# The second experts in two parts of two sequences

## The chip, the cores and the metric

One core of a Trainium2 chip. The metric is the device time of one execution in microseconds (us). PE is the matrix engine (TensorE), DVE VectorE, ACT ScalarE, POOL GpSimd and SP SyncE, which here only issues DMAs. Each engine works through its own queue in order and waits on counting semaphores.

## The reference

Four sequences of 512 tokens with 128 channels pass two layers. Both layers modulate with values from a conditioning vector (scale, shift and gate per sequence). Layer 0 is a state-space mixer and eight experts with two of eight chosen. Layer 1 is causal attention with 16 heads and a second set of eight experts, which the change is about:

```python
logits = flat @ Wr                                            # 2048 tokens, 8 experts
top_vals, top_idx = jax.lax.top_k(logits, TOP_K)              # TOP_K = 2
weights = jax.nn.softmax(top_vals, axis=-1)
top1 = top_idx[:, 0]
h = jax.nn.gelu(jnp.einsum('td,edh->teh', flat, W1), approximate=False)   # 128 -> 512
y = jnp.einsum('teh,ehd->ted', h, W2)                         # 512 -> 128
out = weights[:, 0] * y[top1]                                 # in short: the best expert's row alone
```

The kernel computes for each token the one best expert e with the weight w = 1 / (1 + exp(second - best)). So each token belongs to one expert, and which one is known only at run time.

## The kernel before, in words

All work of layer 1 follows orders written out by hand, one for each engine.

**The attention** goes in 16 groups of four heads, four per sequence, in a loop over `it` (-2 to 16) with eight slots `i` each. In iteration `it` PE computes the scores of group `it + 2` (`scores`, L1641) for the row maxima, which DVE takes (`maximum`, L1221); POOL splits the maxima of group `it + 1` in three bf16 parts in four small operations (`max_parts`, L522 to L528); PE transposes them in slot 2 (`maxima_T`, L1651), ACT copies them (L817) and SP stores them as extra rows of the queries (L364); and PE computes the transposed scores of group `it` with them subtracted (`scores_T`, L1667, L1672), ACT exponentiates (`probs`, L778), and PE weights the values (`weighted_values`, L1686). A group's output goes through ACT (L811), a transpose (`o_T`, L1695) and a division (`o_norm`, L1233, L1237); after a sequence's four groups come a transpose (`a_T`, L1702), the output projection (`attn_out`, L1710) and the sum into x (L1243). Scores, projections and transposes share three PSUM banks in turn, the ring: a bank is taken again when its reader is done. In iterations 4, 5, 8 and 9 POOL issues the copies of the next sequences' queries and keys (`late_relayout`, L317), two groups of four DMAs per iteration, each after the landing of the one before.

**The router's input** of a sequence is x normalized (`ln_stats`, `ln_moments`, `ln_rstd` L399 and L401, `ln_apply` L406), scaled and shifted (`router_input`). For sequences 0 to 2 POOL does this in iterations 10 to 15, for the last one DVE after the attention.

**The second experts** begin when the attention has ended. PE transposes the input of all four sequences (L1367) and forms the logits (L1509), DVE chooses the largest (L1088 to L1092), and PE counts with two products (L1750, L1751) the rank of each token in its expert. From these DVE works out blocks of 128 rows, each of one expert (at most 16 + 8 - 1 = 23), the place of each token (`posu`) and the expert of each block (L1275 to L1292). POOL stores the 16 tiles of tokens at their places in HBM (L586), SP loads the blocks (L370), and then come 23 blocks:

```python
pool.indirect_dma_start(out=slots_x[:, :], out_offset=bass.IndirectOffsetOnAxis(
    ap=posu[:, t:t + 1], axis=0), in_=rows[:, t, :], in_offset=None).then_inc(sem("scattered"), 16)
...
v.tensor_copy(w1[:, j % 2, :], w["W1"][:, bass.ds(at_w, HID)]).then_inc(sem("w1"), 1)
v.tensor_copy(xT[:, j % 2, :], ps[:, 2 + j % 2, 0:P]).then_inc(sem("xT"), 1)
...
mm = pe.matmul(ps[:, 6 + j % 2, 0:D], gs[:, j % 2, q * P:(q + 1) * P],
               w["W2"][:, bass.ds(at_w[j] + q * D, D)], start=(q == 0), stop=(q == 3))
```

In a block step PE transposes the next block (L1762), computes this one's hidden layer (L1771) and the previous one's output (L1782); ACT applies gelu (L838); DVE copies the next block's weights and input (L1319, L1321) and the previous output (L1325), and a gate row of the first 16 steps (L1329). POOL stores each block's 128 results back by token (L592, the return stores). When all are back, SP loads them (L373), each sequence is multiplied and added (`combine`, L413, L415), and SP stores the output (L381).

## Time and profile before

| | us |
|---|---|
| median of 3 runs (579.58 to 580.09) | 580.0 |
| profiled execution | 577.07 |
| its span, first to last instruction | 575.2 |
| PE busy | 452.4 (79%) |
| DVE busy | 392.0 (68%) |
| ACT busy | 278.1 (48%) |
| POOL busy | 271.6 (47%) |
| mean granted clock of PE, full is 1 | 0.889 |

The span is 1.87 us shorter than the profiled execution's own time, and that execution is 2.9 us below the median of the runs. Busy shares are averages over stages of different kinds; the attention's loop lies roughly between 300 and 463 us, the blocks of the second experts between 510 and 558.

### The profile page before, as it was taken

How to read it: one execution, taken by the hardware profiler on the slowest of the kernel's cores; microseconds unless marked ns; L12 is line 12 of the kernel's file. 1: busy time of each engine (PE TensorE's matmuls, PEld its weight loads, DVE VectorE, ACT ScalarE, POOL GpSimd, SP SyncE). 2: the span in 40 equal slices, each digit the busy share in tenths (PEclk: the TensorE clock that was granted, in tenths of full speed). 3: DMA queues.
4: the chain of work that ended last, by engine and by line, in shares of the span. 5: the costliest groups of instructions: out<-in, count | busy, mean ns of one | idle time of the engine just before them, and what ended most of it. 6: DMA issues, size and time to landing. Idle time of an engine off the chain costs nothing.

```text
span 575.2 us, 10088 instructions
## 1 busy us (share of the span) xinstructions
PE 452.4 (79%) x3120; PEld 274.4 (48%) x3120; DVE 392.0 (68%) x1264; ACT 278.1 (48%) x518; POOL 271.6 (47%) x392
## 2 busy tenths in 40 slices
PE   3688778987998999994558998999999863059970
PEld 3545456766653444442323434435445343049970
DVE  5789738988655888886679687888898235025533
ACT  1568796653453544441223577678777831013220
POOL 4210038998301786664641047476655502714541
PEclk9988889999799999997775799999999985559995
DMA  8600000000335333310386012222300000141114
GB/s 354 169 1 1 0 2 2 1 2 1 144 148 125 99 106 99 107 62 2 108 208 124 4 31 88 82 86 85 84 5 4 3 0 10 52 123 36 36 38 146
DMA packets 25739, 39.94 MB, mean 69 GB/s; under 512 B 3228, under 2 KB 17756, under 8 KB 25164
## 3 DMA queue, kind: packets, MB, share of 16 engines
q1 hardware_dynamic: 21752, 30.42, 17.8%
q0 software_dynamic: 3936, 8.89, 5.2%
q8 instruction: 26, 0.43, 0.3%
q14 instruction: 25, 0.20, 0.1%
HBM read 27.55 MB, written 11.55 MB: 68 GB/s over the span
## 4 chain that ended last, share of the span: by engine, by line
PE 49%; DVE 18%; POOL 11%; issue 8%; ACT 6%; DMA 6%; SPq 0%; DVEq 0%; POOLq 0%; ACTq 0%
PE ps L1579 5%; PE ps L1581 5%; PE ps L1568 5%; PE ps L1686 4%; PE ps L1599 3%; PE ps L1771 3%; PE ps L1782 3%; POOL slots_x L586 3%; DVE rows L406 3%; PE ps L1391 2%; DVE moe L1221 2%; PE ps L1641 2%; POOL qk_parts L305 2%; DVE st L387 2%; PE ps L1672 2%
## 5 line engine op out<-in xcount | busy, mean ns | idle before, releaser
L1221 DVE CUSTOM_DVE_ANT_0 moe<-ps,const 128x512 bf16<-128x512 f32 (+3 forms) x256 | 110.5, 486 | 9.7 <-PE ps L1641 9.4
L778 ACT ACTIVATE arena<-ps 128x256 f32<-128x256 f32 (+3 forms) x128 | 85.8, 701 | 33.6 <-PE ps L1672 32.9
L476 POOL TENSOR_TENSOR arena<-arena 128x512 f32<-128x512 f32 x32 | 51.7, 1616 | 51.9 <-DVE arena L1139 51.7
L1641 PE MATMUL ps<-arena 48*128 48x128 bf16 (+3 forms) x256 | 56.1, 329 | 10.7 <-DVE arena L1221 4.7
L1672 PE MATMUL ps<-arena 51*128 51x128 bf16 (+3 forms) x256 | 52.2, 307 | 0.0
L1686 PE MATMUL ps<-arena 128*32 128x512 f32 (+3 forms) x512 | 48.4, 450 | 0.9 <-ACT arena L778 0.6
L1667 PE MATMUL ps<-bconst 64*128 64x64 bf16 x512 | 45.6, 195 | 1.2 <-ACT arena L778 0.5
L1641 PEld LDWEIGHTS ps<-arena 48*128 48x128 bf16 x256 | 16.7, 97 | 55.7 <-DVE arena L1221 31.7
L751 ACT ACTIVATE arena<-arena 128x512 f32<-128x512 f32 x32 | 20.2, 630 | 41.9 <-DVE arena L1139 41.6
L838 ACT ACTIVATE arena<-ps 128x512 f32<-128x512 f32 x23 | 13.7, 597 | 55.0 <-PE ps L1771 55.0
L592 POOL DMA_INDIRECT tokens_y<-arena,token_at x23 | 22.1, 960 | 32.5 <-DVE arena L1325 31.3
L950 DVE SCALAR_TENSOR_TENSOR arena<-ps,mixw,arena 128x511 f32<-128x511 f32 (+2 forms) x48 | 33.1, 737 | 5.2 <-ACT arena L643 5.2
L1667 PEld LDWEIGHTS ps<-bconst 64*128 64x128 bf16 x512 | 29.5, 97 | 12.0 <-ACT arena L778 4.5
L1579 PE MATMUL ps<-arena,moe 128*128 128x512 f32 x64 | 32.8, 593 | 1.8 <-DVE arena L1122 1.8
L441 POOL TENSOR_TENSOR arena<-arena 128x256 f32<-128x256 f32 x16 | 12.4, 776 | 44.4 <-DVE arena L933 40.5
L1581 PE MATMUL ps<-arena,moe 128*128 128x512 f32 x64 | 32.7, 592 | 0.0
L1568 PE MATMUL ps<-arena,moe 128*128 128x512 f32 x64 | 32.5, 592 | 0.0
L1130 DVE SCALAR_TENSOR_TENSOR arena<-ps,moe,arena 128x512 f32<-128x512 f32 x32 | 24.0, 751 | 12.3 <-PE ps L1581 12.2
L1762 PE MATMUL ps<-const,arena 128*128 128x128 f32 x23 | 6.5, 293 | 29.1 <-DMA arena<-slots_x 29.1
L1367 PE MATMUL ps<-const,rows 128*128 128x128 f32 x64 | 13.8, 367 | 17.6 <-DVE rows L406 14.9
L1771 PE MATMUL ps<-arena 128*128 128x128 f32 x184 | 26.5, 290 | 0.6 <-DVE arena L1321 0.5
L1139 DVE SCALAR_TENSOR_TENSOR arena<-ps,moe,arena 128x512 f32<-128x512 f32 x32 | 24.0, 751 | 3.5
(239 smaller groups left out, 1113.2 us busy)
## 6 DMA issues: line engine op xcount, KB each, us to landing
arena<-expert_weights SPq DMA_DIRECT2D x32, 256.0 KB, 3.2
arena<-moe_in SPq DMA_DIRECT2D x1, 4100.0 KB, 12.8
qk_parts<-arena SPq DMA_DIRECT2D x24, 128.0 KB, 2.3
qk_parts<-arena POOLq DMA_DIRECT2D x24, 128.0 KB, 2.3
arena<-qk_parts POOLq DMA_DIRECT2D x32, 96.0 KB, 2.5
arena<-qk_parts SPq DMA_DIRECT2D x8, 288.0 KB, 5.6
moe<-moe_in SPq DMA_DIRECT2D x1, 1936.0 KB, 13.8
slots_x<-zeros SPq DMA_DIRECT2D x1, 1518.0 KB, 19.6
```

What stands on the lines that cost most here:

```text
L476: pool.tensor_tensor(yacc[:, ts], yacc[:, ts], pr[:, i % 2, :], ALU.add).then_inc(sem("yacc"), 1)
L778: act.activation(pt[:, u % 4, :, 0:n], ps[:, 4 + 2 * k:6 + 2 * k, 0:n], ACT.Exp, scale=ATT_SCALE).then_inc(sem("probs"), 1)
L950: v.scalar_tensor_tensor(out=acc[b % 2][:, c, s:S], in0=ps[:, c, 0:S - s], scalar=w["conv_w"][:, 4 * c + 3 - s:4 * c + 4 - s], in1=acc[b % ...
L1221: v.tensor_tensor_reduce(out=junk[:, done % 2, 0:n], in0=ps[:, k, col:col + n], in1=w["mask"][:, (3 - qt) * P:4 * P], scale=1.0, scalar=3 ...
L1568: pe.matmul(ps[:, 6 + i % 2, :], w["w2"][:, e * D:(e + 1) * D], gT[:, i % 2, :], start=True, stop=True).then_inc(sem("p2_ps"), 1)
L1579: pe.matmul(ps[:, 2 + i % 2, :], w["w1"][:, e * D:(e + 1) * D], xm[:, i % 2, :], start=True, stop=True).then_inc(sem("p1_ps"), 1)
L1581: pe.matmul(ps[:, 4 + i % 2, :], w["w3"][:, e * D:(e + 1) * D], xm[:, i % 2, :], start=True, stop=True).then_inc(sem("p3_ps"), 1)
L1641: mm = pe.matmul(ps[:, k, col:col + n], qaug[lo:lo + KR, b % 2, 2 * g + j // 2, qt * P:(qt + 1) * P], kaug[lo:lo + KR, b % 2, 2 * g + j // ...
L1667: pe.matmul(ps[:, bank, HALF * qh:HALF * (qh + 1)], w["causal"][lo:lo + HALF, qh * P:(qh + 1) * P], w["half"][lo:lo + HALF, :], start=(qh ...
L1672: mm = pe.matmul(ps[:, bank, 0:n], kaug[lo:lo + KM, b % 2, 2 * g + jp, kt * P:(kt + 1) * P], qaug[lo:lo + KM, b % 2, 2 * g + jp, kt * P:S] ...
L1686: mm = pe.matmul(ps[32 * j:32 * j + 32, 3, kt * P:S], va[:, b % 2, kt, 4 * (s % QG) + j, :], pt[:, (2 * m + j // 2) % 4, j % 2, 0:n], star ...
L1771: mm = pe.matmul(ps[:, j % 2, q * P:(q + 1) * P], w1[:, j % 2, q * P:(q + 1) * P], xT[:, j % 2, :], start=True, stop=True)
```

## The change

The second experts run in two parts of two sequences each (`PARTS = 2`, eight token tiles, `PT`). A part has up to 8 + 8 - 1 = 15 blocks, so there are 30 block steps in all.

- The first part (sequences 0 and 1) is routed inside the attention. PE transposes its inputs in (11, 6) and (12, 1) of (iteration, slot), forms the logits in (12, 4) and the ranks in (13, 4); ACT copies the transposes; DVE chooses in (12, 5) and computes blocks and positions in (13, 5) to (13, 7). POOL normalizes sequence 0 in iterations 8 to 10 instead of 10 and 11, sequence 1 in 10 and 11 instead of 12 and 13, sequence 2 from 13; its eight row stores follow its last split of maxima.
- When the attention has ended, the first part's blocks start. Between them stand the last group's output, the last sequence's input, and the routing of the second part (sequences 2 and 3). Its eight row stores stand behind eight of the first part's return stores on POOL.
- The first part's results are loaded, combined (both sequences on POOL) and stored while the second part's blocks run.
- Outputs go over the block's own input in `xb` instead of a buffer of their own; the last iteration (16) of the attention's loop is written out; some semaphores are shared (the wait for one load becomes a wait for three); the small routing tiles lie in the space of the mixer's weights; HBM space for 30 blocks is cleared instead of 23.

```diff
-NBLK = NT + E1 - 1
+PARTS = 2
+PT = NT // PARTS
+NBLK = PT + E1 - 1
...
+        ROUTER_AT = {(11, 6): ("h4T", 0), (12, 1): ("h4T", 1), (12, 4): ("logits", 0), (13, 4): ("ranks", 0)}
...
-            sp.wait_ge(sem("scattered"), 16 * NT)
-            slots = slots_x.rearrange("(j p) d -> p j d", p=P)
-            for c, js in enumerate(BLOCK_GROUPS):
-                sp.dma_start(xb[:, js, :], slots[:, js, :]).then_inc(sem(f"ld_moe1_{c}"), 16)
-            sp.wait_ge(sem("returned"), 16 * NBLK)
...
+            slots = slots_x.rearrange("(a j p) d -> a p j d", p=P, a=PARTS)
+            for a in range(PARTS):
+                sp.wait_ge(sem(f"scattered{a}"), 16 * PT)
+                if a == 0:
+                    sp.wait_ge(sem("pv"), 4 * QG * (B - 1))
+                for c, js in enumerate(BLOCK_GROUPS):
+                    sp.dma_start(xb[a][:, js, :], slots[a, :, js, :]).then_inc(sem(f"ld_slots{a}{c}"), 16)
+            for a in range(PARTS):
+                sp.wait_ge(sem(f"returned{a}"), 16 * NBLK)
...
-                if it >= 10:
-                    b, half = divmod(it - 10, 2)
-                    for step in ((0,), (1, 2))[half]:
-                        router_input(b, step)
+                if it == 8:
+                    router_input(0, 0)
+                elif it == 9:
+                    router_input(0, 1)
+                elif it == 10:
+                    router_input(0, 2)
+                    router_input(1, 0)
+                elif it == 11:
+                    router_input(1, 1)
+                    router_input(1, 2)
+                elif it == 13:
+                    router_input(2, 0)
...
+            def to_slots(a):
+                pool.wait_ge(sem("posu"), a + 1)
+                pool.wait_ge(sem("h4"), 2 * (a + 1))
+                if a == 0:
+                    pool.wait_ge(sem("slots_clear"), 16)
+                for t in range(PT * a, PT * (a + 1)):
+                    pool.indirect_dma_start(out=slots_x[:, :], out_offset=bass.IndirectOffsetOnAxis(
+                        ap=posu[:, t:t + 1], axis=0), in_=rows[:, t, :], in_offset=None)\
+                        .then_inc(sem(f"scattered{a}"), 16)
+            def to_tokens(a, j):
...
+            to_slots(0)
             router_input(2, 1)
             router_input(2, 2)
             ln_rstd(pool, 4, B - 1)
-            pool.wait_ge(sem("posu"), 1)
...
-            for t in range(NT):
-                pool.indirect_dma_start(out=slots_x[:, :], out_offset=bass.IndirectOffsetOnAxis(
-                    ap=posu[:, t:t + 1], axis=0), in_=rows[:, t, :], in_offset=None).then_inc(sem("scattered"), 16)
+            for j in range(RETURNED_FIRST):
+                to_tokens(0, j)
+            to_slots(1)
+            for j in range(RETURNED_FIRST, NBLK):
+                to_tokens(0, j)
             for j in range(NBLK):
...
+                to_tokens(1, j)
+                if j in (4, 7):
+                    if j == 4:
+                        pool.wait_ge(sem("gate_weights"), PT)
+                    b = (j - 4) // 3
+                    combine(pool, b, "y_weighted0", "x4_pool", b + 1)
...
+                    if (it, i) == (12, 5):
+                        choose(0)
+                    elif (it, i) == (13, 5):
+                        expert_blocks(0)
+                    elif (it, i) == (13, 6):
+                        positions(0)
+                    elif (it, i) == (13, 7):
+                        block_experts(0)
+                        second_best(0)
+                    elif (it, i) == (14, 2):
+                        top_weight(0)
...
+            def block_step(i):
+                if i % 5 == 0 and i < 2 * NBLK:
+                    block_tokens(i)
+                if i + 1 < 2 * NBLK:
+                    weights_in(i + 1)
+                    if (i + 1) % NBLK > 0:
+                        block_in(i + 1)
+                block_out(i - 1)
+                if (i + 1) % NBLK == 0:
+                    block_out(i)
+                    if i + 1 < 2 * NBLK:
+                        block_in(i + 1)
+            weights_in(0)
+            block_in(0)
+            o_norm(NT - 1)
+            weights_in(1)
+            block_in(1)
+            block_tokens(0)
+            weights_in(2)
+            block_in(2)
+            attn_out(B - 1)
+            router_input(B - 1, 0)
+            router_input(B - 1, 1)
+            block_out(0)
+            router_input(B - 1, 2)
+            router_input(B - 1, 3)
+            block_step(2)
+            router_input(B - 1, 4)
+            block_step(3)
+            for i in range(4, 7):
+                gate_weights(2 * (i - 4))
+                gate_weights(2 * (i - 4) + 1)
+                block_step(i)
+            choose(1)
+            block_step(7)
+            expert_blocks(1)
+            block_step(8)
+            positions(1)
+            block_step(9)
+            block_experts(1)
+            second_best(1)
+            for i in range(10, NBLK):
+                if i < 12:
+                    gate_weights(i - 4)
+                block_step(i)
+            weights_in(NBLK + 1)
+            block_in(NBLK + 1)
+            block_tokens(NBLK)
+            for i in range(NBLK + 1, PARTS * NBLK):
+                block_step(i)
+            top_weight(1)
+            for t in range(PT, NT):
+                gate_weights(t)
             v.wait_ge(sem("gate_weights"), NT)
-            for b in range(1, B):
-                combine(v, b, "y_weighted", "x4", b)
+            combine(v, B - 1, "y_weighted", "x4", 1)
...
+            weighted_values(4 * NT - 1)
             pe.wait_ge(sem("probs"), 128)
-            pe.wait_ge(sem("ld_moe1"), 16)
-            router(4, w["wr"], "gate1_ps")
-            pe.wait_ge(sem("route"), ROUTE1)
...
-            pe.wait_ge(sem("expert_at"), 1)
...
+            ring_free(pe, 2, RING_MAIN)
+            block_in(0)
+            o_T(NT - 1)
+            h4_T(2)
+            block_in(1)
+            block_hidden(0)
+            a_T(B - 1)
+            block_step(1)
+            attn_out(B - 1)
+            for i in range(2, 6):
+                block_step(i)
+            h4_T(3)
+            block_step(6)
+            logits(1)
+            block_step(7)
+            ranks(1)
+            for i in range(8, NBLK):
+                block_step(i)
+            block_in(NBLK + 1)
+            block_hidden(NBLK)
+            for i in range(NBLK + 1, PARTS * NBLK):
+                block_step(i)```

In PE's queue after the attention the `router` function and the loop over 23 blocks are gone; `block_step(i)` of PE is the transpose of block i + 1, the hidden layer of i and the output of i - 1, and at the end of a part both outputs before the next part's first transpose.

**POOL around iterations 8 and 9.** Before:

```order
L522 CAST arena<-arena 128x16
L524 TENSOR_TENSOR arena<-arena 128x16
L526 CAST arena<-arena 128x16
L528 TENSOR_TENSOR arena<-arena 128x16
L317 DMA arena<-qk_parts 48x2x512 x8
L522 CAST arena<-arena 128x16
L524 TENSOR_TENSOR arena<-arena 128x16
L526 CAST arena<-arena 128x16
L528 TENSOR_TENSOR arena<-arena 128x16
L317 DMA arena<-qk_parts 48x2x512 x8
L522 CAST arena<-arena 128x16
```

Now (L553 to L559 are the split of maxima, L344 the copies, L430 to L437 the normalization, L570 and L575 scaling and shifting):

```order
L344 DMA arena<-qk_parts 48x2x512 x8
L430 TENSOR_SCALAR rs<-mv 128x4
L432 TENSOR_TENSOR rs<-rs,neghalf 128x4
L437 TENSOR_SCALAR rows<-x,mv,rs 128x128 x4
L553 CAST arena<-arena 128x16
L555 TENSOR_TENSOR arena<-arena 128x16
L557 CAST arena<-arena 128x16
L559 TENSOR_TENSOR arena<-arena 128x16
L344 DMA arena<-qk_parts 48x2x512 x8
L570 TENSOR_TENSOR rows<-rows,mod 128x4x128
L553 CAST arena<-arena 128x16
L555 TENSOR_TENSOR arena<-arena 128x16
```

The normalization of sequence 0 stands between iteration 8's copies and the split of iteration 9, and its scaling before the split of iteration 10.

**DVE at the end of iteration 13.** The rows L1302 are maxima, 512 wide in slot 6; the change puts these seven rows (positions) behind them and before the maxima of slot 7, and five such rows (L1360 to L1366, blocks) before slot 6:

```order
L1302 ISA moe,arena<-ps,const 128x512
L1302 ISA arena 128x1
L1370 TENSOR_TENSOR mixw<-mixw 128x8
L1371 TENSOR_TENSOR mixw<-mixw 128x64
L1372 SCALAR_TENSOR_TENSOR mixw<-mixw 128x64
L1374 TENSOR_TENSOR mixw<-mixw 128x64
L1375 TENSOR_TENSOR mixw<-mixw 128x64
L1376 TENSOR_REDUCE mixw<-mixw 128x8
L1377 TENSOR_SCALAR posu<-mixw 128x8
L1302 ISA moe,arena<-ps,const 128x384
```

Before, rows like these stood behind the whole attention.

**POOL from the last split of maxima on.** Before, 16 row stores and 23 return stores stood one behind the other; now:

```order
L559 TENSOR_TENSOR arena<-arena 128x16
L624 DMA slots_x<-rows,posu 3840x132 x8
L570 TENSOR_TENSOR rows<-rows,mod 128x4x128
L575 TENSOR_TENSOR rows<-rows,mod 128x4x128
L430 TENSOR_SCALAR rs<-mv 128x4
L432 TENSOR_TENSOR rs<-rs,neghalf 128x4
L633 DMA tokens_y<-arena,token_at 5889x128 x8
L624 DMA slots_x<-rows,posu 3840x132 x8
L633 DMA tokens_y<-arena,token_at 5889x128 x12
L444 TENSOR_TENSOR arena<-arena 128x512
L446 TENSOR_TENSOR x<-x,arena 128x512
```

L624 are the row stores, L633 the return stores, L444 and L446 the first combination.

## Rows read from the trace of the kernel before

**Rows 1.** The page, part 2: granted clock in 40 slices of 14.4 us, tenths

```profile
PEclk9988889999799999997775799999999985559995
```

**Rows 2.** Windows: length; busy PE, PEld, DVE, ACT, POOL; clock, DMA share, GB/s

```profile
430.00:438.00 8.00, 7.96 (x108) 4.27 (x108) 7.04 (x31) 6.34 (x12) 5.26 (x10) 1.00 0.01 2
438.00:448.60 10.60, 9.98 (x136) 5.10 (x131) 9.85 (x51) 7.34 (x12) 3.42 (x7) 1.00 0.01 4
471.10:510.10 39.00, 5.60 (x24) 5.18 (x24) 9.70 (x32) 2.11 (x3) 15.55 (x17) 0.50 0.14 45
516.30:559.00 42.70, 41.56 (x365) 40.59 (x363) 22.65 (x84) 12.55 (x21) 21.13 (x23) 1.00 0.10 34
```

**Rows 3.** Chain that ended last, first block on PE: start, us, what

```profile
510.13 0.46 PE ps L1762
```

**Rows 4.** Timeline of POOL, iterations 9 to 11: start, us, what [idle <-releaser]

```profile
405.31 0.23 POOL L522 CAST arena<-arena 128x16 bf16<-128x16 f32 x1
...
412.78 2.24 POOL L317 DMA_DIRECT2D arena<-qk_parts  x4 [2.89 <-DMA arena<-qk_parts]
...
416.08 0.23 POOL L399 TENSOR_SCALAR rs<-mv 128x4 f32<-128x4 f32 x1
...
417.55 3.16 POOL L406 TENSOR_SCALAR rows<-x,mv,rs 128x128 f32<-128x128 f32 x4
...
423.74 1.27 POOL L539 TENSOR_TENSOR rows<-rows,mod 128x512 f32<-128x512 f32 x1
```

**Rows 5.** Timeline of PE, transposes of maxima in iterations 9 and 10

```profile
407.25 0.39 PE L1651 MATMUL ps<-bconst,arena 128*12 128x128 bf16 x4
...
416.17 0.39 PE L1651 MATMUL ps<-bconst,arena 128*12 128x128 bf16 x4 [0.39 <-POOL arena L528]
```

**Rows 6.** Timeline of all engines, end of the attention and router

```profile
461.99 1.06 PE L1686 MATMUL ps<-arena 128*32 128x512 f32 x8 [0.60 <-ACT arena L778]
...
463.77 0.66 PE L1695 MATMUL ps<-const,mod 128*128 128x128 f32 x4 [0.72 <-ACT mod L811]
...
468.73 1.06 PE L1509 MATMUL ps<-arena,hT 128*128 128x8 f32 x8 [0.25 <-ACT hT L831]
...
482.79 0.17 DVE L1281 TENSOR_TENSOR arena<-arena 128x8 f32<-128x8 f32 x1
```

**Rows 7.** Timeline of DVE, the last maximum of the attention

```profile
448.21 0.29 DVE L1221 CUSTOM_DVE_ANT_0 moe<-ps,const 128x128 bf16<-128x128 f32 x1
```

**Rows 8.** Row stores on the timeline; return stores by line, with ns min/median/max

```profile
485.26 1.14 POOL L586 DMA_INDIRECT slots_x<-rows,posu  x1 [14.15 <-DVE posu L1288]
...
504.41 0.96 POOL L586 DMA_INDIRECT slots_x<-rows,posu  x1 [0.31 <-issue]
...
L592 POOL DMA_INDIRECT tokens_y<-arena,token_at x23: 956/960/962, 516.9 to 559.0; - x23
```

**Rows 9.** Timeline, blocks: hidden layers on PE and a weight copy on DVE

```profile
511.12 2.05 PE L1771 MATMUL ps<-arena 128*128 128x128 f32 x8 [0.33 <-DVE arena L1321]
...
521.03 0.43 DVE L1319 COPY arena<-arena 128x512 f32 x1 [0.38 <-issue]
...
521.97 1.06 PE L1771 MATMUL ps<-arena 128*128 128x128 f32 x8
```

**Rows 10.** Timeline of POOL, its combination of one sequence

```profile
564.24 1.26 POOL L413 TENSOR_TENSOR arena<-arena 128x512 f32<-128x512 f32 x1 [4.29 <-DMA arena<-tokens_y]
...
565.58 1.59 POOL L415 TENSOR_TENSOR x<-x,arena 128x512 f32<-128x512 f32 x1
```

**Rows 11.** Timeline of POOL, first step of each split of maxima

```profile
314.72 0.21 POOL L522 CAST arena<-arena 128x16 bf16<-128x16 f32 x1 [6.83 <-DVE arena L1221]
...
325.80 0.21 POOL L522 CAST arena<-arena 128x16 bf16<-128x16 f32 x1 [9.99 <-DVE arena L1221]
...
422.68 0.21 POOL L522 CAST arena<-arena 128x16 bf16<-128x16 f32 x1 [1.97 <-DVE arena L1221]
...
430.65 0.22 POOL L522 CAST arena<-arena 128x16 bf16<-128x16 f32 x1 [4.29 <-DVE arena L1221]
```

469 lines of the change are left out of this document (269 added, 200 removed).

## The prediction

> **What bounds the kernel now.** I read the slices first: the clock row is near full speed through the attention and falls to half in slices 34 to 36, after it [rows 1]. The windows put numbers on that hole. From 471.1 to 510.1 us PE has 5.6 us of work in 39 [rows 2], and from 510.1 the 23 blocks of the second experts run one after the other, PE busy for 41.6 us of 42.7 [rows 2]. In the hole stands a serial chain: last attention output, normalization, router logits, choice, ranks, positions, then 16 row stores on POOL, 1.28 us apart (485.26 to 504.41), and 5.7 us from the last one's start until PE has the first block [rows 3, 8]. The attention before it is close to full: in 430 to 438 us PE is busy for 7.96 of 8.0 us, in the iteration after that DVE for 9.85 of 10.6 [rows 2]. So the change takes work out of a nearly empty place and puts some of it into a nearly full one, and it runs 30 blocks where 23 were.
>
> **The sum** follows one path through four places. The profiled execution took 577.07 us with a span of 575.2; the median of the three runs is 580.0. I sum against the span and subtract the difference from the median. About 0.2% (1.2 us) is what a measurement can tell from no change.
>
> *1. POOL in iteration 8 to 10: +4.8 us.* The normalization of sequence 0 (from 416.08 to 420.71, 4.6 us [rows 4]) moves two iterations forward. There it stands behind the two groups of copies of iteration 8 and ahead of the split of maxima that started at 405.31. This starts at 409.9. PE's transposes follow the start of a split by 1.2 us (415.0 to 416.17), so PE, which transposed these maxima at 407.25 [rows 5], waits until 411.1. Behind it come eight DMA issues with the wait of 2.9 us between them (2 x 2.24 + 2.89) and now a scaling of 1.3 us [rows 4]. So the next split, which began when the second four had been issued at 412.78 + 2.24 = 415.0, begins at 411.0 + 7.4 + 1.4 = 419.8, and PE's transposes of 416.17 move to 421.0 [rows 5]. The copies' own wait for DMAs is unchanged, and no scores wait for them: they are needed from iteration 10. All of PE's in-order queue stands behind that transpose. Lower bound: PE and DVE catch up some of it, since PE waited for DVE about 1 us here; upper 5.5.
>
> *2. PE in iterations 11 and 12: +3.4.* Two sets of four transposes at 0.66 and logits of eight token tiles, twice the 1.06 of four [rows 6]. PE has no room there [rows 2], so they add up. The choice on DVE, six small operations (under 2 us), lies in the 0.96 us that DVE has left plus what PE's extra work leaves it. ACT's two copies lie beside it. Bounds: 1.5 if the idle bits of PE take them up, 4.5 if PE also waits for ACT to free a bank of the ring.
>
> *3. DVE in iteration 13: +2.4.* Before the last four maxima of the attention stand twelve small operations (blocks and positions). Operations of 8 elements take 0.17 [rows 6], those of 128 elements 0.29 [rows 7]; with the gaps I take 0.26 for 64 elements, 3.1 us in all. DVE has 0.75 us idle in this iteration [rows 2]. The last maximum at 448.5 [rows 7] sets when POOL can split it, and from that PE, ACT, SP and a DMA follow before PE gets the last group. Nothing covers it. The two rank products on PE (under 0.5) lie behind DVE here. Bounds 1.5 and 3.5.
>
> The attention's last product, which ends at 463.05 [rows 6], then ends at 463.05 + 4.8 + 3.4 + 2.4 = **473.6**.
>
> *4. Row stores of the first part: the end of attention no longer waits for them, nearly.* The last maximum is done at 459.1, POOL splits it until 460.5, eight stores start 1.28 us apart, the last at 469.4, and 5.7 us later, at **475.1**, PE has block 0 [rows 3, 8]. PE waits 1.5 us, and the transposes of the last output, which stand behind block 0 in its queue, wait too.
>
> *5. From block 0 to block 15: 46.8.* This is what used to be the hole for one sequence pair, now with 15 blocks in its gaps. PE's order from block 0: last output, transposes of sequence 2, two hidden layers of 0.9, one output, attention projection: 6.8 us until x of the last sequence. Statistics, moments, root on POOL, scaling and shifting with one block step's copies between them: 6.7. Then DVE must do steps 3 to 6 with gate rows and token rows while PE does blocks, transposes and the logits (2.1): 9.4. Choice, step, blocks, step, positions on DVE, each step 1.25 us of DVE's copies: 1.6 + 1.25 + 1.4 + 1.25 + 1.75 = 7.3. Eight stores, landing and load: 14.7. That is 44.9; POOL's first eight returns are done by then. I add 1.9 for the clock: PE idles some 4 us while DVE normalizes the last sequence, and the first hidden layer after the hole took 2.05 us with the clock at half, where later ones take 1.06 [rows 9]. Bounds 43 and 55. PE's own work on blocks 2 to 14 (13 x 1.91 = 24.8) ends a little before, so the blocks are free. Block 15 enters PE at **521.9**.
>
> *6. The second part: 33.0.* Before, 48.85 us lie between the first block's start and the last return's (510.13 to 558.98 [rows 3, 8]). A block takes (559.0 - 516.9) / 22 = 1.91 [rows 8]; eight fewer leave 33.55, with a slow start that I halve (-1.3), and POOL now also combines two sequences among its returns: 2 x 2.85 us [rows 10], of which its 0.6 us of room per block takes up all but some 0.7. The last return starts at **554.9**.
>
> *7. The end: 13.8.* It was 16.2 (558.98 to 575.2). Two sequences instead of four are left, one on each engine: 2.4 less. Sum **568.7**, 6.5 below 575.2. Early edits (one wait for three loads, a clearing store of 30 blocks instead of 23, at the start) cost nothing: their consumers start over 100 us later.
>
> **A rule weighed.** The 23 return stores took 0.96 us each with DVE's f32 copies beside them, and the 16 stores of rows 0.96 with DVE idle [rows 8, 9]. I therefore give the second part's stores no extra time. The Trainium skill says in "SBUF — State Buffer", section "SBUF: two separate sides", that a DMA issued from POOL cannot write its descriptors while DVE holds the shared ports for an f32 copy. By that rule each of the eight stores would wait for up to one copy of 0.43, and the sum would be 572.1; the rows here show nothing of it.
>
> **The rivals.**
> *A, the attention has more room (0.25).* For it: PE's busy time is modelled, and several small waits lie in it. Places 1 to 3 then cost 5 instead of 10.6, and place 5 needs no 1.9: 580.0 - 6.5 - 7.5 = 566.
> *B, the clock falls in the attention (0.14), slower.* PE's new wait of 4 us at 407.3 is the mechanism; the clock row is at half where PE had gaps before the attention, and there one iteration took 11.1 us (314.72 to 325.80) where a later one takes 8.0 (422.68 to 430.65 [rows 11]). Each iteration at half speed costs 3.1 us; seven remain. From three on the kernel is slower than before: 573.5 + 3 x 3.1 = 583, all seven 595. Against it: dense work brought the clock back each time, and 2 us of the loss hide in the second POOL wait. The Trainium skill ("TensorE: Matmul & The Clock Gate", "What's actually happening") says that the clock follows how busy the array has been; that is the direction of this rival, and the trace agrees that gaps precede each fall.
> *C, the last sequence's chain is held up between the blocks (0.14).* DVE's queue alternates block copies and routing, each waiting for PE. If PE stays at half clock through the first steps, a step takes 3.8 instead of 2.7, and eight of them stand before the second positions: +7, 580.5. For it: the gaps of place 5. Against: in the gaps a block's work is at hand most of the time.
> *D, the first part's stores come late (0.05).* If the positions miss iteration 13, the stores start an iteration later and the cover is lost: +6, 579.5.
>
> **How the numbers follow.** My forecast has 0.42: 580.0 - 6.5 = 573.5 us. Range 564 to 584: down to A with two us to spare, up over C and D and the first quarter of B, which leaves some 0.2 out. Faster: the forecast's case but for 0.03, A, and 0.08 of C and D: 0.72. Same (578.8 to 581.2): 0.07. Slower: B and the rest of C: 0.21.
>
> **What would show it.** After it, the split of maxima for iteration 10 starts near 410, not 405, and PE has one wait of about 4 us there; the attention's last product ends near 473.6; block 0 enters PE within 2 us of that, not 47 us later; positions of the second part come near 505, block 15 near 522; the last return starts near 555, and 13.8 us are left. The forecast is wrong at place 1 if PE's wait is small, at 5 if block 15 enters after 530, and as a whole if PE is not the engine that the attention's end follows. The clock row tells B and C.

## The result: slower by 4.1% where 1.1% faster was forecast

The changed kernel takes 603.0 us (median of four runs, 600.6 to 606.13) against 579.8 for the kernel before beside it (577.23 to 580.09): a ratio of 1.0414, 95% interval 1.0354 to 1.0474. 573.5 was forecast, 564 to 584; the time lies far outside, on the side that had 0.21.

The profiled execution took 600.6 us with a span of 598.6, 23.4 more than before. The places of the forecast, read from its trace (us):

| stretch | before | forecast | after |
|---|---|---|---|
| first split of maxima to the start of the last weighted values | 155.2 | 165.8 | 184.3 |
| from there to block 0 on PE | 48.1 | 2.6 | 1.0 |
| block 0 to block 15 | - | 46.8 | 54.2 |
| block 15 to the last return store | 48.85 (all 23 blocks) | 33.0 | 33.4 |
| last return store to the end | 16.2 | 13.8 | 16.9 |

The first split starts at 306.79 before and at 308.80 after. Over all traces of this study it lies between 306.8 and 311.6, in the code of the kernel before as well, so I measure the attention from it. The first nine distances between splits are scattered too: no edit of an experiment but the unread products of e14 and e15 touches the instructions there, and they add up to 88.2 to 89.5 us in all other traces but one (91.0 in e11). A difference of 1 us in the attention's whole length can come from there. What the change was to remove it removed (48.1 to 1.0). The attention took 29 us more for it where 10.6 were reckoned, and the first 15 blocks 7 more than reckoned.

The page's busy rows and chain, beside the granted clock of [rows 1]:

```profile
PE   3696878987999999966579989997989676957970
...
PEclk9887799998999999996756999997997569997995
...
PE 50%; DVE 19%; POOL 9%; issue 7%; ACT 7%; DMA 3%; another core or an unknown queue 2%; DVEq 1%; SPq 0%; POOLq 0%; ACTq 0%
```

"Another core or an unknown queue" stands on a page of a single core; the page of before has no such entry. It comes back below.

Windows (columns as in [rows 2]): POOL's work of place 1 and what follows it, the stretch behind the logits of place 2, the end of the attention, the first part's blocks, the second part's.

```profile
410.00:412.00 2.00, 0.00 (x0) 0.00 (x0) 0.00 (x0) 0.00 (x0) 1.85 (x4) 1.00 0.00 0
412.00:420.00 8.00, 7.26 (x66) 3.68 (x66) 4.29 (x23) 3.55 (x5) 4.93 (x10) 0.57 0.27 74
...
446.00:456.00 10.00, 10.00 (x62) 5.69 (x61) 4.74 (x22) 3.46 (x4) 0.87 (x4) 0.51 0.01 2
476.00:490.00 14.00, 8.98 (x80) 2.98 (x78) 0.55 (x2) 5.67 (x9) 6.17 (x6) 0.50 0.34 98
495.00:548.00 53.00, 38.35 (x295) 36.20 (x296) 24.97 (x98) 11.82 (x19) 21.90 (x23) 0.90 0.15 47
560.00:580.00 20.00, 17.98 (x155) 17.27 (x154) 11.26 (x29) 5.79 (x10) 13.93 (x13) 1.00 0.16 57
```

POOL's timeline for place 1, against [rows 4], and the wait on PE against [rows 5]:

```profile
408.32 3.16 POOL L437 TENSOR_SCALAR rows<-x,mv,rs 128x128 f32<-128x128 f32 x4
411.42 0.21 POOL L553 CAST arena<-arena 128x16 bf16<-128x16 f32 x1
...
421.49 0.21 POOL L553 CAST arena<-arena 128x16 bf16<-128x16 f32 x1
```

```profile
412.58 0.59 PE L1815 MATMUL ps<-bconst,arena 128*12 128x128 bf16 x4 [4.09 <-POOL arena L559]
```

It is as foretold: less the 2.0 of the later start, the two splits are 4.1 and 4.5 us later than before (405.31, 415.0), or 5.0 and 5.3 if the first nine distances, 0.9 shorter here, are left out, and PE has its one wait of 4 us. But from here the clock is at half speed (0.57 in the window above). Place 2, on PE's timeline: PE's products for the scores wait for ACT, which copies the transposes of the router's input and so frees their ring bank late, and the logits of eight tiles take 2.42 where two of [rows 6] would be 2.12:

```profile
438.40 0.37 PE L1805 MATMUL ps<-arena 48*128 48x512 bf16 x1 [0.91 <-ACT hT L873]
...
442.87 0.33 PE L1805 MATMUL ps<-arena 48*128 48x384 bf16 x1 [1.32 <-ACT hT L873]
...
444.85 2.42 PE L1896 MATMUL ps<-arena,hT 128*128 128x8 f32 x16
```

The last part of the attention, all engines:

```profile
467.13 0.17 DVE L1377 TENSOR_SCALAR posu<-mixw 128x8 uint32<-128x8 f32 x1
...
469.87 0.17 DVE L1392 TENSOR_TENSOR mixw<-mixw 128x8 f32<-128x8 f32 x1
470.06 0.21 ACT L877 ACTIVATE mixw<-mixw 128x8 f32<-128x8 f32 x1 [3.54 <-DVE mixw L1392]
...
470.54 1.14 POOL L624 DMA_INDIRECT slots_x<-rows,posu  x1 [0.58 <-issue]
470.60 0.13 PEld L1831 LDWEIGHTS ps<-bconst 64*128 64x128 bf16 x4 [3.50 <-ACT arena L836]
...
479.26 1.51 PE L1850 MATMUL ps<-arena 128*32 128x384 f32 x8
479.58 0.96 POOL L624 DMA_INDIRECT slots_x<-rows,posu  x1 [0.30 <-issue]
...
482.07 2.21 ACT L836 ACTIVATE arena<-ps 128x1024 f32<-128x1024 f32 x3 [3.50 <-remote]
...
493.10 1.07 PE L1850 MATMUL ps<-arena 128*32 128x512 f32 x8 [0.97 <-ACT arena L836]
494.10 0.33 PE L1946 MATMUL ps<-const,arena 128*128 128x128 f32 x1
```

Two things stand here that the forecast did not have. ACT's small exponential of the routing (L877) waits for DVE's last small operation, and with it, in ACT's in-order queue, the exponentials of the scores (L836), for which PE waits 3.5 us. And at 482.07 ACT is released by something "remote". The rows beside the second part's row stores show that more plainly (PE, ACT and DVE beside POOL):

```profile
526.52 0.96 POOL L624 DMA_INDIRECT slots_x<-rows,posu  x1 [0.71 <-DVE posu L1377]
...
530.02 0.43 DVE L1433 COPY arena<-arena 128x512 f32 x1 [0.57 <-issue]
...
530.32 0.96 POOL L624 DMA_INDIRECT slots_x<-rows,posu  x1 [0.30 <-issue]
...
530.70 1.16 PE L1957 MATMUL ps<-arena 128*128 128x128 f32 x8 [1.05 <-issue]
...
531.70 1.06 PE L1966 MATMUL ps<-arena 128*128 x8
...
535.38 0.96 POOL L624 DMA_INDIRECT slots_x<-rows,posu  x1 [0.31 <-issue]
536.57 0.60 ACT L883 ACTIVATE arena<-ps 128x512 f32<-128x512 f32 x1 [7.29 <-remote]
...
537.31 1.16 PE L1966 MATMUL ps<-arena 128*128 x8 [3.55 <-ACT arena L883]
...
540.86 0.29 DVE L1451 COPY arena<-ps 128x128 f32<-128x128 f32 x1 [9.16 <-remote]
```

PE's hidden layer is recorded as done at 531.86; ACT, idle, begins to read it at 536.57, 4.7 us later. PE's output is done at 532.76; DVE, idle, copies it at 540.86, 8.1 later. ACT is the one who goes on first, 0.2 us after the record of the last row store has ended; two return stores follow at once, and DVE goes on 2.0 us after the second of them (537.91 to 538.87). "Remote" is the name that the profile gives a release that fits no record in time. I call this a **hold-up**: what PE's products release comes late, and everyone in the loop of PE, ACT and DVE stands. In the trace of before there is none.

The end, against the 16.2 of before:

```profile
581.70 0.96 POOL L633 DMA_INDIRECT tokens_y<-arena,token_at  x1 [0.30 <-issue]
...
588.37 1.59 POOL L446 TENSOR_TENSOR x<-x,arena 128x512 f32<-128x512 f32 x1
588.87 1.63 DVE L446 TENSOR_TENSOR x<-x,arena 128x512 f32<-128x512 f32 x1
590.53 0.83 SPq L412 DMA_DIRECT2D y_out<-x  x2
```

### The profile page after: what moved, and what is told of

The parts are those of the page before. It is cut to its first block, busy times and chain, and to the rows that moved or that the text cites. A ratio compares the mean times of both kernels' runs of the same rounds, so it can differ in the third digit from the quotient of the medians.

```text
span 598.6 us, 10516 instructions
## 1 busy us (share of the span) xinstructions
PE 480.3 (80%) x3243; PEld 292.2 (49%) x3243; DVE 404.5 (68%) x1312; ACT 283.9 (47%) x527; POOL 284.3 (47%) x403
## 2 busy tenths in 40 slices
PE   3696878987999999966579989997989676957970
## 3 DMA queue, kind: packets, MB, share of 16 engines
q1 hardware_dynamic: 23576, 31.33, 19.2%
## 4 chain that ended last, share of the span: by engine, by line
PE 50%; DVE 19%; POOL 9%; issue 7%; ACT 7%; DMA 3%; another core or an unknown queue 2%; DVEq 1%; SPq 0%; POOLq 0%; ACTq 0%
PE ps L1850 5%; PE ps L1746 5%; PE ps L1735 5%; PE ps L1748 5%; PE ps L1764 3%; PE ps L1836 3%; PE ps L1957 3%; PE ps L1805 2%; DVE rows L437 2%; DVE moe L1302 2%; PE ps L1573 2%; PE ps L1966 2%; POOL qk_parts L332 2%; DVE st L418 2%
## 5 line engine op out<-in xcount | busy, mean ns | idle before, releaser
L1302 DVE CUSTOM_DVE_ANT_0 moe<-ps,const 128x512 bf16<-128x512 f32 (+3 forms) x256 | 110.9, 486 | 19.9 <-PE ps L1805 19.6
L836 ACT ACTIVATE arena<-ps 128x256 f32<-128x256 f32 (+3 forms) x128 | 86.4, 701 | 51.8 <-PE ps L1836 47.8
L1805 PE MATMUL ps<-arena 48*128 48x128 bf16 (+3 forms) x256 | 57.1, 335 | 13.8 <-DVE arena L1302 5.3
L1836 PE MATMUL ps<-arena 51*128 51x128 bf16 (+3 forms) x256 | 55.4, 329 | 0.0
L1850 PE MATMUL ps<-arena 128*32 128x512 f32 (+3 forms) x512 | 53.9, 497 | 1.0 <-ACT arena L836 1.0
L1831 PE MATMUL ps<-bconst 64*128 64x64 bf16 x512 | 46.9, 201 | 7.3 <-ACT arena L836 6.8
L883 ACT ACTIVATE arena<-ps 128x512 f32<-128x512 f32 x30 | 17.9, 598 | 62.0 <-PE ps L1957 33.8
L1805 PEld LDWEIGHTS ps<-arena 48*128 48x128 bf16 x256 | 17.0, 98 | 58.4 <-DVE arena L1302 31.1
L1957 PE MATMUL ps<-arena 128*128 128x128 f32 x240 | 34.6, 290 | 13.5 <-DVE arena L1438 8.7
L633 POOL DMA_INDIRECT tokens_y<-arena,token_at x30 | 29.4, 979 | 33.2 <-DVE arena L1451 29.9
L1831 PEld LDWEIGHTS ps<-bconst 64*128 64x128 bf16 x512 | 30.3, 100 | 22.3 <-issue 8.8
L1957 PEld LDWEIGHTS ps<-arena 128*128 128x128 f32 x240 | 30.7, 200 | 16.4 <-DVE arena L1438 10.6
L1966 PE MATMUL ps<-arena 128*128 x240 | 33.2, 284 | 3.7 <-ACT arena L883 3.6
L1966 PEld LDWEIGHTS ps<-arena 128*128 128x128 f32 x240 | 30.6, 200 | 4.2 <-issue 4.0
L1211 DVE SCALAR_TENSOR_TENSOR arena<-ps,moe,arena 128x512 f32<-128x512 f32 x32 | 24.0, 751 | 12.0 <-PE ps L1748 12.0
```

The source lines that it names most:

```text
L836: act.activation(pt[:, u % 4, :, 0:n], ps[:, 4 + 2 * k:6 + 2 * k, 0:n], ACT.Exp, scale=ATT_SCALE).then_inc(sem("probs"), 1)
L1302: v.tensor_tensor_reduce(out=junk[:, done % 2, 0:n], in0=ps[:, k, col:col + n], in1=w["mask"][:, (3 - qt) * P:4 * P], scale=1.0, scalar=3 ...
L1805: mm = pe.matmul(ps[:, k, col:col + n], qaug[lo:lo + KR, b % 2, 2 * g + j // 2, qt * P:(qt + 1) * P], kaug[lo:lo + KR, b % 2, 2 * g + j // ...
L1831: pe.matmul(ps[:, bank, HALF * qh:HALF * (qh + 1)], w["causal"][lo:lo + HALF, qh * P:(qh + 1) * P], w["half"][lo:lo + HALF, :], start=(qh ...
L1836: mm = pe.matmul(ps[:, bank, 0:n], kaug[lo:lo + KM, b % 2, 2 * g + jp, kt * P:(kt + 1) * P], qaug[lo:lo + KM, b % 2, 2 * g + jp, kt * P:S] ...
L1850: mm = pe.matmul(ps[32 * j:32 * j + 32, 3, kt * P:S], va[:, b % 2, kt, 4 * (s % QG) + j, :], pt[:, (2 * m + j // 2) % 4, j % 2, 0:n], star ...
```

## The experiments

Expectations are in times of the run or in differences against the changed kernel. "Relative end" is the stretch of the table's first line: 155.2 before, 184.3 after. Of every kernel one execution was traced; lengths inside a kernel are that execution's, times are medians of 4 to 12. Jobs ran on different chips, and each has its own runs of the kernel before: e1 to e4 on one chip (before 579.1), e5 to e8 on another (577.8), e9 to e11 (577.9), e12 to e15 (578.1) and e16 to e18 (578.3) on three more. Ratios are against those.

### First question: which addition lengthens the attention?

**e1: the first part's routing behind the attention; e2: POOL's normalization in its old iterations as well.**

```diff
-        ROUTER_AT = {(11, 6): ("h4T", 0), (12, 1): ("h4T", 1), (12, 4): ("logits", 0), (13, 4): ("ranks", 0)}
+        ROUTER_AT = {}
...
+            h4_T(0)
+            h4_T(1)
+            logits(0)
+            ranks(0)
```

(likewise the calls on DVE and ACT; in e2 also `if it >= 10: b, half = divmod(it - 10, 2)` of before)

> The changed kernel, but the transposes, logits and ranks of the first part, their copies and the choice, blocks and positions stand behind the attention's last product; POOL's order is the changed one. If the pieces on PE, DVE and ACT in iterations 11 to 14 cost the attention most of its 31 us (theory R), its last product starts near 469 (461.99 before, + 2.0 from ahead of the attention, + 4.5 for POOL's part); it then takes some 24 us until block 0, so the whole is near the 603 of the changed kernel, 598 to 606. If POOL's moved normalization costs most of it (theory P), the last product starts after 480 and the whole is over 610.

> As e1, and POOL's normalization stands where it stood before the change (iterations 10 to 14). Both theories: last product of the attention near 464 (before: 461.99; 2.0 were already lost at the attention's start in the changed kernel's trace). The whole is 4.5 to 6 us below e1 if the wait of 4 us behind POOL and the clock's fall after it cost what the trace suggests; equal to e1 within 1 if they are taken up later. Its distance to the kernel before (580) is what the blocks in two parts cost by themselves.

Measured: e1 604.6, ratio 1.0446 (1.0402 to 1.0491); e2 596.8, 1.0295 (1.0269 to 1.0322). Relative ends 160.9 and 155.7. So POOL's earlier normalization costs 160.9 - 155.7 = 5.2 us (6.4 without the first nine distances), and all else in the attention 184.3 - 160.9 = 23.4. With nothing in the attention it has the length of before again, and two parts are then still 3% slower: 30 blocks, a chain that no longer lies inside, and a hold-up, which e2 has beside the second part's row stores too (DVE idle for 9.0 until 536.46).

Part of e1's cost stands at a place that the forecast did not look at. POOL now normalizes sequence 2 in iteration 13, one iteration earlier than before, and the last split of maxima stands right behind it (e1, POOL; in e2 and before this split waits for DVE alone):

```profile
453.02 3.12 POOL L438 TENSOR_SCALAR rows<-x,mv,rs 128x128 f32<-128x128 f32 x4
456.10 0.20 POOL L554 CAST arena<-arena 128x16 bf16<-128x16 f32 x1
```

The distance between the last two splits is 10.8 in e1 and 9.5 in e2: 1.3 us. In the changed kernel the last split waits 2.1 us longer for DVE, so nothing of it shows there.

**e3: POOL's normalization nearly back, the routing stays in, but PE's second transposes and the logits stand two slots and one slot later; e4: the second row stores in pairs, with one return store between.**

```diff
-                if it == 8:
+                if it == 10:
...
-                elif it == 9:
+                elif it == 11:
```

```diff
-            to_slots(1)
...
+                if j < 12:
+                    to_slots(1, 2 * (j - 8), 2 * (j - 8) + 2)
```

> The changed kernel, but POOL normalizes sequence 0 in iterations 10 and 11 and sequence 1 in 11 and 12, behind the splits that followed a long wait; PE's second transposes and logits stand two slots and one slot later. Theory P: PE's wait of 4 us at 408 and the half clock at 412 to 419 go, 5 to 8 us less: 595 to 598. Theory R: at most 4.5 less, and iterations 12 and 13 still lose 13 us against before.

> The changed kernel, but the second part's eight row stores go in four pairs with a return store of the first part behind each, instead of eight in a row. In the trace ACT stood 7.3 us and DVE 9.2 us while the eight went out, with nothing of the kernel to wait for. If a long unbroken run of POOL's stores is what holds them (theory S), those two waits shrink below 3 us, block 15 is on PE near 541 instead of 548.3, and the whole is near 596. If it is a thing of their own queues at that place in the program, they stay, at the same instructions, and the whole is 602 to 605.

e3: 594.2, 1.0257 (1.0233 to 1.0281), relative end 175.6: the 5.2 of POOL and more are back, 8.7 in all. That is more than theory R allowed (4.5), and the attention still loses 20.4 against before, so neither theory had it alone; which of the two edits gave the rest was not separated. e4: 603.5, 1.0403 (1.0365 to 1.044), as the changed kernel. Its trace has the same hold-ups; the returns in between were ready, so the first eight stores still followed each other every 1.26 to 1.27 us, and the edit made no gap until the hold-up was there. It says nothing on gaps.

### Second question: the hold-ups and the exponential

**e5: the changed kernel with a POOL operation of 512 elements (1.28 us), awaited, behind each row store; e6: e3 with the routing's exponential behind the last scores; e8: e6 with e5's operations.** e7 is the kernel before with its first return stores held back until 12 are ready, so that they go out in one run beside PE's blocks.

```diff
+                    pool.tensor_tensor(pause[:, 0:512], pause[:, 512:1024], pause[:, 1024:1536], ALU.add)\
+                        .then_inc(sem("paused"), 1)
+                    pool.wait_ge(sem("paused"), t + 1)
```

```diff
-                    if (it, i) == (13, 7):
-                        top_exp(0)
...
+            top_exp(0)
```

```diff
-                pool.wait_ge(sem("pr"), DENSE + j + 1)
+                pool.wait_ge(sem("pr"), DENSE + max(j + 1, 12))
```

> The changed kernel, with one extra POOL operation of 512 elements (some 1.3 us, on a tile that is no longer used) behind each of the 16 row stores, so that no run of stores is unbroken. Seen so far: in six traces the semaphores that PE's matmuls raise arrive late by 2 to 7 us, and only while POOL's row stores (8 in a row, 1.27 us apart) go out beside PE's work; they arrive again 1.4 to 2.0 us after the last store of the run. Theory S (an unbroken run of POOL's stores withholds PE's results): no ACT or DVE wait without a cause over 1.5 us is left in the whole second half, and the attention's last product starts 4 to 5 us earlier, near 489. The stores themselves take 20 us instead of 10, so block 0 and block 15 may wait for them: the whole 596 to 604. Rival (it is the stores' number or their target, not the missing pause): the waits stay at 3 us or more each.

> e3 (POOL's normalization later, 594.2), and ACT's exponential of 8 values of the first part moves from iteration 13 to behind the attention. In e3 ACT stood 3.54 us at it, waiting for DVE's small operations behind the last maxima, and PE's next scores 2.73 us behind ACT. If that wait is on the path: 2.5 to 3.5 less, 591; if the row stores' start (463.6), which does not depend on it, and the late results of PE set the end of the attention: within 1 of e3.

> The kernel before the change, but POOL holds its return stores until block 11 is out and then issues them one behind the other beside PE's blocks. Theory S: PE's results come late by over 3 us while this run lasts (some 15 stores), DVE and ACT wait for nothing visible, the whole is 588 or more. Rival (only row stores, or only the changed kernel): PE's results arrive in time; 23 stores at 1.27 us from 534 end at 563 instead of 559, so 582 to 585.

> e6 and e5's pauses together. Under theory S the attention's last product starts near 477 (485.1 in e3, less 3 for the exponential, less 4.9 for the late results); the stores start near 460 and end near 481, so block 0 waits for them until 487: the whole 586 to 592. Without theory S: 594 to 598, since the stores are only longer.

Measured: e5 606.5, 1.0508 (1.0463 to 1.0553); e6 593.0, 1.0278 (1.0235 to 1.0321); e7 594.4, 1.0288 (1.0246 to 1.0329); e8 598.1, 1.0354 (1.0313 to 1.0394). The pauses take the hold-ups away: e5 and e8 have no "remote" release from 465 to 560 us, while e6, which differs from e8 in the pauses alone and ran on the same chip, has four there, up to 8.72. But a pause of 1.28 after each of 16 stores costs more than it saves: e8 is 5.1 slower than e6, and both e5 and e8 miss what was expected of them (596 to 604, 586 to 592). In e7, whose code is that of before but for the held stores, hold-ups appear (ACT and DVE beside the return stores, which follow each other every 1.26 us):

```profile
547.27 0.60 ACT L838 ACTIVATE arena<-ps 128x512 f32<-128x512 f32 x1 [3.02 <-remote]
...
551.58 0.29 DVE L1325 COPY arena<-ps 128x128 f32<-128x128 f32 x1 [5.67 <-remote]
...
557.99 0.60 ACT L838 ACTIVATE arena<-ps 128x512 f32<-128x512 f32 x1 [10.13 <-remote]
...
559.52 0.96 POOL L592 DMA_INDIRECT tokens_y<-arena,token_at  x1 [0.30 <-issue]
563.03 0.29 DVE L1325 COPY arena<-ps 128x128 f32<-128x128 f32 x1 [10.08 <-remote]
```

Relative ends: e5 175.9, without hold-ups but with all of the routing, and e8 167.4. Both hold the scatter of the first nine distances, so I read the prices from the stretch in which the two causes stand, from the last split of maxima to the last weighted values. It is 13.4 before, 24.3 in the changed kernel and 16.3 in e5; 22.9 in e6 and 14.9 in e8. So the hold-up in the attention costs 8.0 (24.3 - 16.3, and 22.9 - 14.9 by the pauses alone), and the exponential 1.5 (16.3 - 14.9). In e3 against e6 the edit of the exponential shows nothing (1.0257 and 1.0278, each against its own before): where its wait went, a hold-up took its place.

**e9: e8 with short pauses (128 elements), and the ranks on PE and all of DVE's small operations behind the last maxima.**

```diff
-                    elif (it, i) == (13, 5):
+                    elif (it, i) == (13, 7):
                         expert_blocks(0)
-                    elif (it, i) == (13, 6):
                         positions(0)
```

> e6 (593.0) with two edits. The pause behind each row store is one POOL operation of 128 elements (some 0.4 us, so stores 1.7 us apart, 14 us for eight), and the ranks of the first part on PE and all of DVE's small operations behind them move behind the last maxima of iteration 13. Theory D (they hold up the last maxima): the last split of maxima is 3 us earlier relative to the one before it (14.6 apart in e8, 14.8 in e6), and the attention's last product starts near 474.5 (477.6 in e8). Theory S asks how short a pause may be: with 0.4 us no semaphore of PE late by over 1.5 us, or late ones again by 3 us and more. The whole 584 to 588 if both hold, 590 to 595 if the results of PE are late again.

586.2, 1.0127 (1.0089 to 1.0165), relative end 164.6: 2.8 less than e8, or 3.8 without the first nine distances, the price of place 3. Of the 3.8, 2.3 fall before the last split and so ahead of every store: the last two distances add up to 26.5 instead of 28.8. The other 1.6 fall behind it, from 14.9 to 13.3. It has no hold-up, but it ran on a third chip, on which the next run has none without any pause; so how short a pause may be is not shown.

**e11: e1 with 16 unread products on PE while it waits for POOL in iteration 9 to 10** (it adds work that nothing reads).

```diff
+                if s == 10:
+                    for _ in range(16):
+                        pe.matmul(ps[:, k, 0:448], identb, bconst[:, 0:448], start=True, stop=True,
+                                  skip_group_check=True)
                 pe.wait_ge(sem("m_parts"), 4 * (s + 1))
```

> e1 (POOL's normalization early, routing behind the attention; 604.6, last product 469.4) with 16 products of 448 columns that nobody reads, on PE while it waits for the split of maxima of iteration 9 (about 4 us idle, after which the granted clock fell to 0.50 until 419). If the half clock behind that wait costs time, the clock stays at 1.00, the last product starts 1 to 3 us earlier, 466.5 to 468.5, and the whole is 601 to 603.5. If only the wait itself counts: within 0.7 of 469.4 and 604.6, or later by what the products take beyond the wait.

597.7, 1.033 (1.029 to 1.0371). Windows of its trace, columns as above:

```profile
409.00:412.00 3.00, 3.00 (x24) 1.46 (x21) 2.34 (x12) 1.09 (x3) 2.89 (x5) 1.00 0.05 14
412.00:416.00 4.00, 3.36 (x45) 1.98 (x43) 1.20 (x6) 1.09 (x2) 3.51 (x9) 1.00 0.11 32
...
424.00:428.00 4.00, 4.00 (x42) 2.07 (x39) 2.75 (x14) 2.13 (x4) 3.81 (x6) 0.57 0.03 7
```

The clock stays full where it fell in e1, and one split later the gain is half a microsecond (9.59 us between the two splits that are 10.06 apart in e1); at 424 the clock falls after all, and the next distance is 9.1 instead of 8.0. The relative end is 164.3, against 160.9 of e1; 2.8 of these 3.4 lie in the first nine distances, ahead of the products, so the products changed the rest by no more than 0.6. Holding the clock over POOL's 4 us gives back next to nothing of what the wait costs; the later fall, with PE at work, goes with 1.1 more. The whole is 7 us below e1, outside both expectations: this run, on a third chip and with no pauses, has no hold-up.

### Third question: a version that gains

**e10: the routing in iterations 13 and 14 where the attention thins out, normalization as before, the last sequence's chain ahead of the blocks, short pauses. e12: the same with both parts' row stores in one piece each, the chain's steps moved up, and no pauses behind return stores. e13: e12 without the pauses.**

```diff
-        ROUTER_AT = {(11, 6): ("h4T", 0), (12, 1): ("h4T", 1), (12, 4): ("logits", 0), (13, 4): ("ranks", 0)}
+        ROUTER_AT = {(13, 7): ("h4T", 0), (14, 0): ("h4T", 1), (14, 2): ("logits", 0), (14, 4): ("ranks", 0)}
...
-            block_in(0)
             o_T(NT - 1)
+            a_T(B - 1)
+            attn_out(B - 1)
             h4_T(2)
+            h4_T(3)
+            block_in(0)
             block_in(1)
             block_hidden(0)
-            a_T(B - 1)
             block_step(1)
-            attn_out(B - 1)
```

> What the runs so far ask for, on the changed kernel: POOL's normalization as in e3, with sequence 2 done in iteration 14; the first part's transposes, logits and ranks on PE and all its small operations on DVE in iteration 14, where no maxima are left; behind the attention first the last sequence's output, normalization and both its transposes, then block 0; the second part's routing between steps 1 and 4; row stores and the first part's return stores with a pause of one small POOL operation behind each. Expected: the attention's last product near 466 (463.2 in e2, plus the routing in a half empty iteration), stores from 463 to 478, block 0 near 483, second positions near 490, block 15 near 513 (15 steps of 1.91, if no PE result is late), last return 546, end 563; with 2 around it 565, 560 to 572. If PE's results are late again: 575 to 585. If the routing costs the attention what it did in iterations 12 and 13 (14 us): 575.

> e10 (585.3) with the order behind the attention mended: POOL issues all eight row stores of the first part before it waits for the last sequence's moments (in e10 that wait split them, 10 us), the second part's logits stand behind two transposes of blocks and its ranks behind step 1, DVE's choice and positions likewise, and no return store stands between the second part's row stores (in e10 they took 504.7 to 521). Expected: stores of the first part 461 to 475, block 0 near 482, second positions near 492, stores to 506, block 15 near 514, POOL behind with its returns: last return 547 to 550, whole 566 to 570. If PE's results are late beside POOL's returns (which have no pause here): 572 to 578.

> e12 without the pauses behind the row stores: each run of eight takes 10 us instead of 14. If PE's results stay in time: block 0 near 478, block 15 near 511, 2 to 4 below e12. Theory S as it stands (any unbroken run withholds them): late by over 3 us beside both runs, 5 to 10 above e12.

Measured: e10 585.3, 1.013 (1.0093 to 1.0167); e12 575.1, 0.9944 (0.9909 to 0.9979); e13 574.2, 0.9927 (0.9892 to 0.9962). Relative ends 162.1, 160.6 and 161.5, so all of the routing costs about 6 us in iteration 14 (the three traces against e2), where in iterations 11 to 13 it costs 14.4 (e5, e14, e17 and e18 against e1; both without the first nine distances). e10 missed its 560 to 572: block 0 starts at 488.1 where 483 was expected and block 15 at 527.8 where 513 was, and with a pause behind most of the first part's return stores POOL's operations follow each other from 522.6 to the last return within 0.31 us. The rest of e12's gain over e10 lies behind the attention: block 0 starts 13.0 us after the last weighted values instead of 19.1, and from block 0 to the last return it takes 73.1 us instead of 77.8 (87.6 in the changed kernel), all of it behind block 15, where it is 32.4 instead of 38.1. e12 in turn missed its 566 to 570; block 15 starts at 524 where 514 was expected. e13 is 0.9 below e12, which the noise does not tell from nothing. **e13 is faster than before** by 0.7% (interval 0.4 to 1.1), and by 4.7% than the change if each is set against its own before. Part of the 4.7 is that no kernel of e13's job had a hold-up: e14 below, the changed kernel but for unread products that lengthen it by 3.8 us, takes 589.7 on that chip, 2.7% more than e13, or 2.0% without the products. Nor has e13 a hold-up, though its row stores follow each other as in the changed kernel: so an unbroken run of stores isn't enough.

### Fourth question: does PE's stream of instructions decide?

The page of the changed kernel counts the packets of a queue that brings instructions, and in the DMA records one of them comes for about every 254 of PE's 7120 rows (3243 products, as many weight loads, and 634 of its sequencer):

```profile
q8 instruction: 28, 0.46, 0.3%
```

One theory was that a hold-up comes when such a fetch falls into a run of stores. Products that nothing reads shift it: 16 (e14) or, at PE's very start, 128 (e17) or 64 (e18), where each product is two rows of PE's stream; e15 shifts e7 by the 16 of e14. e16 is e13 with both first blocks inside the last sequence's normalization and POOL's second row stores ahead of its first return stores.

```diff
+                if s == 0:
+                    for _ in range(16):
+                        pe.matmul(ps[:, k, 0:448], identb, bconst[:, 0:448], start=True, stop=True,
+                                  skip_group_check=True)
```

```diff
+            for _ in range(128):
+                pe.matmul(ps[0:16, 7, 0:16], zb[:, 0:16], zb[:, 128:144], start=True, stop=True,
+                          skip_group_check=True)
```

```diff
-            for step in range(5):
-                router_input(B - 1, step)
+            router_input(B - 1, 0)
+            router_input(B - 1, 1)
             weights_in(0)
-            block_in(0)
             weights_in(1)
+            router_input(B - 1, 2)
+            block_in(0)
```

> The changed kernel (603.0) with 16 products that nobody reads on PE, where it waits for the first split of maxima, 200 us ahead of any row store. Theory S (the run of stores alone): nothing changes, 602 to 605, PE's results late by 4.9 and 7.2 us at the same instructions. Theory I (a run of stores and the place in PE's stream of instructions): at least the second hold-up (ACT 7.3 us, DVE 9.2 us) is gone or stands at other instructions; the whole 594 to 598 if gone.

> e7 (the kernel before with held return stores, 594.4) with the same 16 products. Theory S: 593 to 596, hold-ups as in e7. Theory I: the hold-ups (two, 8 us and 10 us long) move or vanish: 580 to 588.

> e13 (574.2) with the 6 us filled in which PE waited for DVE's normalization of the last sequence (478 to 484), after which its clock was at half until 492 and the 16 products of the logits took 3.56 us instead of 1.9: blocks 0 and 1 and the first hidden layer now stand ahead of the last transposes, the logits behind step 1, the ranks behind step 2; and POOL issues the second part's row stores ahead of the first return stores. If that gap and its half clock were worth what the windows show: 4 to 6 less, 568 to 570. If the chain of the second part is the bound: within 2 of 574. A new hold-up of PE's results would show as 4 to 8 more.

> The changed kernel (603.0, hold-ups at 478 to 482 and 531 to 541) with 128 products of 16 columns on PE at the very start, while it waits for the first operand: 256 more rows of PE. They may cost up to 5 us there. If what counts is the place within the 256 rows (16 KB) that PE's instruction queue fetches at a time: both hold-ups are back at the same instructions (late by 4.9 and 7.2 us), block 0 to block 15 takes 54, the whole 603 to 608. If not: block 0 to block 15 takes 48 to 49 as in e14, the whole 590 to 595.

> The same with 64 products, 128 rows. By the place within 256: no hold-up at the same instructions, perhaps one at others; block 0 to block 15 in 48 to 50, the whole 590 to 596. If any hold-up stands where it stood in the changed kernel, the place within 256 is not it.

Measured: e14 589.7, 1.0201 (1.0157 to 1.0244); e15 592.0, 1.0217 (1.0171 to 1.0263); e16 576.5, 0.9959 (0.9941 to 0.9978); e17 589.3, 1.019 (1.0145 to 1.0234); e18 588.2, 1.0168 (1.0124 to 1.0213). None has a hold-up in its traced execution. For e15 that settles little: its other three executions took 3.4 to 5.8 us more than the traced one (587.8), and what they had is not known. e16 missed its 568 to 570 and gained nothing over e13: the blocks begin 6.0 us earlier behind the last weighted values, and block 0 to block 15 takes 46.2 instead of 39.8. So the second part's chain is the bound there, as far as one trace of each tells. e17 was to leave the fetches where they were and so keep the hold-ups; it lost them. That speaks against a period of 256, unless the chip alone decides. What e17 shows well is the price: it is the changed kernel but for the products at the start, ACT's exponentials of the scores beside the row stores run through (ACT and POOL),

```profile
473.72 0.96 POOL L624 DMA_INDIRECT slots_x<-rows,posu  x1 [0.30 <-issue]
474.73 1.51 ACT L836 ACTIVATE arena<-ps 128x768 f32<-128x768 f32 x2 [1.54 <-issue]
...
476.82 2.71 ACT L836 ACTIVATE arena<-ps 128x1024 f32<-128x1024 f32 x4 [0.57 <-PE ps L1841]
...
480.66 1.08 ACT L836 ACTIVATE arena<-ps 128x512 f32<-128x512 f32 x2
```

in step with those of the paced e5,

```profile
473.80 1.00 POOL L626 DMA_INDIRECT slots_x<-rows,posu  x1 [0.28 <-POOL mod L629]
474.80 1.51 ACT L841 ACTIVATE arena<-ps 128x768 f32<-128x768 f32 x2 [1.54 <-PE ps L1841]
...
476.88 2.71 ACT L841 ACTIVATE arena<-ps 128x1024 f32<-128x1024 f32 x4 [0.57 <-issue]
...
480.72 1.08 ACT L841 ACTIVATE arena<-ps 128x512 f32<-128x512 f32 x2
```

and it is 13.8 us faster than the changed kernel was. Its relative end is 175.6 (e18 176.0; e14 180.0, of which 3.8 are its products in the first distance), its stretch from block 0 to the last return 83.8 (e18 82.5, e14 81.9) instead of 87.6. From the last split to the last weighted values all three take 16.3, as e5 does.

**What stays open.** Every kernel with hold-ups ran on the chip of e1 to e4 or on that of e5 to e8 (and in the changed kernel's own job, whose chip the result does not name); on the other three chips none had any, neither e15, nearly the same code as e7, nor e13. Whether the chip or the exact stream of PE decides was not separated: the changed kernel itself was not run beside e14, e17 and e18 in one job. Nor do single traces tell whether a kernel's hold-ups stand in each of its executions. Shown is: on one chip pauses of 512 elements between the stores remove hold-ups (e6 against e8); they occur in the kernel before's code too, once its stores go out in a run beside PE's work (e7); and before has none in its trace, in which its 16 row stores go out while PE idles, which fits but was not tried by itself.

## Why the forecast was wrong, place by place

The places are read from the 15 distances between the 16 splits of maxima and the stretch from the last split to the last weighted values (us). The first nine distances are left out; the sum is what remains of the attention.

| | distances 10, 11 | 12, 13 | 14, 15 | behind the last split | sum |
|---|---|---|---|---|---|
| before | 19.1 | 15.6 | 17.9 | 13.4 | 66.0 |
| changed | 24.4 | 16.0 | 31.4 | 24.3 | 96.0 |
| e1, no routing | 24.2 | 16.0 | 19.2 | 13.3 | 72.7 |
| e2, nothing | 19.3 | 15.6 | 17.9 | 13.4 | 66.3 |
| e6 | 19.2 | 15.9 | 29.0 | 22.9 | 86.9 |
| e8, e6 with pauses | 19.5 | 15.9 | 28.8 | 14.9 | 79.1 |
| e9, also place 3 out | 19.6 | 15.9 | 26.5 | 13.3 | 75.3 |
| e5, e14, e17, e18 | 24.1 to 24.5 | 15.6 to 16.0 | 30.0 to 31.4 | 16.3 | 86.4 to 87.8 |

The step that failed is the price of the attention, 10.6 for places 1 to 3: it is 30.0 in the changed kernel and 22.0 without the hold-up. Inside it place 2, PE's own durations of 3.4 with at most 4.5, is 9.0, and ACT's wait and the hold-up stood at nothing.

**1, POOL, +4.8: right.** Distances 10 and 11 grow by 5.3, and by 4.9 in e1 against e2. Missed was sequence 2's normalization ahead of the last split: 1.3 in e1, hidden in the changed kernel.

**2, PE in iterations 11 and 12, +3.4: wrong in size.** It measured 9.0 (e9, which of the attention's additions has only this one left, against e2; its slots are a little later than the changed kernel's, and 1.3 may be POOL's, as in e1). I summed PE's own durations from [rows 6]. That leaves out that each piece holds a ring bank until ACT has copied it, which made PE wait 0.91 and 1.32, and that from 446 to 456 PE is busy without a gap at a clock of 0.51. I wrote that a bank's wait would give 4.5 at most; the upper bound was no bound. How the 9.0 divide between banks and clock was not tried by itself, but the clock seems to have a part. Five kernels have the changed kernel's instructions in distances 14 and 15. They took 30.0 at a mean granted clock of 0.89 (e17) and 30.1 at 0.86 (e5), the changed kernel and e14 and e18 31.3 to 31.4 at 0.80 to 0.84, and e4 34.5 at 0.75; before, these distances ran at 1.00. The same work took longer the lower the clock was; whether the clock is the cause there or follows a longer wait, no run separates.

**3, DVE before the last maxima, +2.4: right in kind,** e8 against e9 gives 3.8, of which 2.3 before the last split. **But a neighbour was missed:** of that stretch I reckoned DVE's operations and PE's, and called ACT's work "beside it". ACT's exponential waits for DVE's small operations and blocks its queue: ACT stands 3.5 us, and the attention is 1.5 longer for it.

**4, block 0 right behind the attention: right.** 1.0 us from the start of the last product, positions done long before (467.13 against 494.10). The longer attention helped: the stores' end, which the forecast had PE wait for, lies far inside it.

**The hold-ups: in no step.** 8.0 us of the attention, and from block 0 to the last return 87.6 - 82.7 (mean of e14, e17 and e18) = 4.9. That is 12.9 of the 23.4 by which the span grew; the medians of e17 and e18 lie 13.8 and 14.8 below the changed kernel's, in other jobs.

**5, block 0 to 15, 46.8: measured 54.2.** Without hold-ups it is 47.8 to 47.9 (e14, e17, e18), 1.1 more than the sum; the other 6.3 are the hold-up.

**6, the second part, 33.0: measured 33.4,** but 34.1 to 35.8 in the three traces without hold-ups, so that the near hit is in part luck. Its stores took 0.96 beside DVE's f32 copies (530.32 beside the copy of 530.02 in the timeline above), so the rule of the Trainium skill ("SBUF — State Buffer", "SBUF: two separate sides") that I set against the sum, by which each such store would wait for a copy, is not seen in these rows either: a store's own record does not grow.

**7, the end, 13.8: wrong, 16.9.** The two combinations fewer are there: the last store moves its data until about 592.9, 11.2 us behind the last return, where before it was about 572.0, 13.0 behind. But from there to the span's end, in which no engine does work of the program, it is 5.7 instead of 3.2. It is 5.7 in all 17 traces of kernels in two parts and 3.2 in all three of the code of before, so the change makes it; what fills it was not tried.

**The rivals.** A (room in the attention) was wrong altogether. B (the clock) named the right side: the clock does fall behind POOL's 4 us, and again later. e11 shows that holding it over that first wait is worth half a microsecond; the later fall, in distances 14 and 15, may have a part in place 2's excess, which no run isolated. C was right in direction by 1 us. D did not occur (stores at 470.54, in iteration 14's last slots as planned). Without hold-ups the change is still slower, by 1.7 and 1.9% (e18, e17), and by 2.0% in e14, where 3.8 us (0.7%) are the products; so it isn't they that turned the sign.

**The sum again.** Without the hold-up and the first nine distances the attention grew by 22.0, 11.4 more than reckoned: 0.5 at place 1, 5.6 at place 2, 1.4 at place 3, 1.5 of the exponential, and 2.4 by which the changed kernel's slots and clock in distances 14 and 15 differ from those of e8, left open. With 1.6 less at 4, 1.1 more at 5, 1.8 at 6 and 3.1 at 7 that is 15.8, which turns a gain of 6.5 into a loss of 9.3. The hold-ups (12.9) and the later first split less the shorter first nine distances (2.0 - 0.9) make it the measured 23.4, to 0.1.

## What to carry to other kernels

A piece of work that goes into a full loop costs more than its duration on its own engine: list for each piece what it holds (a PSUM bank until the copy, an in-order queue until its operand comes) and who stands behind. Put it where the loop thins out: the same routing costs 14 us in iterations 11 to 13 and about 6 in 14, and with the late chain ahead of the blocks that turned 1.3 to 1.9% slower (e14 less its products, e17, e18, none with a hold-up) into 0.7% faster (e13). And read what a page lists as an unknown releaser before anything else when a sum misses.

## What was not expected of the hardware

- While POOL issues indirect stores without a break (every 1.26 to 1.27 us, 8 or more) beside busy PE, what waits for PE's products can be released late: 4.7 and 8.1 us in the changed kernel, with idle stretches of up to 10.1 in e7. Two of the experiments' five chips showed it, in every kernel without pauses that ran there; on one of them an awaited POOL operation of 512 elements behind each store removed it (e6, e8).
- The clock stayed at half speed for 10 us in which PE had no gap at all in the records (446 to 456), behind a stretch in which it had waited twice for banks, 0.91 and 1.32 us.
- Unread products kept the clock at 1.00 through a wait (e11) and brought half a microsecond by the next split.
- From the last output's data to the end of the span it takes 3.2 us in the code of before and 5.7 in every kernel in two parts, with no work of the program recorded.
